# The first expert's first two tiles, filled from eight of sixteen token tiles and run among the convolution's end and the routing

## The reference

```
x = x + conv(ln_c(x))        # 3 causal depthwise convolutions (3, 7, 15 taps), mixed 96 -> 32 by w_mix
t = tokens(x)                # 4 x 512 tokens of 512 features
t = t + moe(layernorm(t))
moe: probs = softmax(x @ gate_w.T); the 2 best of 8 experts, their weights normalised to 1
     h = silu(x @ w1[e]) * (x @ w3[e])    # 512 -> 1024
     y = h @ w2[e]                        # 1024 -> 512, times the gate, summed over the token's experts
```

## Time and profile before

| | |
|---|---|
| median of 3 runs | 844.46 us |
| the profiled execution: its own time | 843.52 us |
| its span, first to last instruction | 841.8 us |
| busy share of the span | PE 94%, VectorE 41%, ScalarE 37%, GpSimd 34% |
| chain that ended last | PE 87%, VectorE 8%, issue 2%, ScalarE 1% |

### The profile page before, as it was taken

The page is one execution under the profiler, slowest core; times in us unless marked ns, Lnnn a source line. Parts: engine busy times, 40 slices in busy tenths (PEclk is TensorE's granted clock), DMA queues, the critical chain, the costliest instruction groups (busy, mean ns, idle before and its releaser), DMA issues.

```text
span 841.8 us, 13004 instructions
## 1 busy us (share of the span) xinstructions
PE 789.8 (94%) x3764; PEld 655.8 (78%) x3765; DVE 347.8 (41%) x791; ACT 314.5 (37%) x487; POOL 286.4 (34%) x313
## 2 busy tenths in 40 slices
PE   4999999639999999999999999999999999999993
PEld 3777888528888888888888888888888888888882
DVE  5887658685113611262117214511361171244111
ACT  6784755433124411352126215312441262253120
POOL 4445220011324522272227215432452272154311
PEclk9999999559999999999999999999999999999997
DMA  7248678728122711272116414612271174111211
GB/s 239 46 76 150 148 153 176 265 98 328 27 35 70 278 37 25 37 285 64 34 29 221 140 25 117 244 27 36 69 280 37 25 232 129 25 25 37 31 32 25
DMA packets 55873, 91.72 MB, mean 109 GB/s; under 512 B 7344, under 2 KB 40496, under 8 KB 49712
## 3 DMA queue, kind: packets, MB, share of 16 engines
q1 hardware_dynamic: 45728, 71.64, 27.4%
q0 software_dynamic: 9408, 19.42, 12.5%
q10 hardware_dynamic: 720, 0.46, 0.2%
HBM read 64.97 MB, written 18.15 MB: 99 GB/s over the span
## 4 chain that ended last, share of the span: by engine, by line
PE 87%; DVE 8%; issue 2%; ACT 1%; DMA 0%; POOL 0%; POOLq 0%; DVEq 0%; ACTq 0%
PE bank L720 23%; PE bank L718 23%; PE bank L719 23%; PE bank L734 4%; PE bank L631 3%; PE bank L632 3%; PE bank L633 3%; PE bank L712 2%; PE bank L653 1%; DVE bn L782 1%; DVE wc_lo L823 1%; DVE w_lo L270 1%; PE bank L671 1%; PE bank L646 1%; DVE mv L791 1%
## 5 line engine op out<-in xcount | busy, mean ns | idle before, releaser
L718 PE MATMUL bank<-w_hi,xT_hi 128*128 128x512 f32 x576 | 228.8, 397 | 4.4 <-DVE xT_lo L1019 4.4
L720 PE MATMUL bank<-w_hi,xT_lo 128*128 128x512 f32 x576 | 225.4, 391 | 0.0
L719 PE MATMUL bank<-w_lo,xT_hi 128*128 128x512 f32 x576 | 225.0, 391 | 0.0
L1042 DVE TENSOR_TENSOR h<-bank,h 128x512 f32<-128x512 f32 x72 | 49.7, 690 | 273.1 <-PE bank L720 273.1
L718 PEld LDWEIGHTS bank<-w_hi,xT_hi 128*128 128x128 f32 x576 | 108.7, 189 | 26.3 <-DVE xT_lo L1019 4.8
L720 PEld LDWEIGHTS bank<-w_hi,xT_lo 128*128 128x128 f32 x576 | 108.5, 188 | 23.5
L719 PEld LDWEIGHTS bank<-w_lo,xT_hi 128*128 128x128 f32 x576 | 108.8, 189 | 21.7
L559 ACT ACTIVATE h<-bank 128x512 f32<-128x512 f32 x72 | 43.0, 598 | 196.6 <-PE bank L720 196.5
L718 PE MATMUL bank<-w_hi,hT_hi 128*128 128x512 f32 x288 | 115.3, 400 | 0.0
L1046 DVE TENSOR_TENSOR hT_lo<-bank,hT_hi 128x512 fp32r<-128x512 f32 x72 | 49.8, 692 | 153.8 <-ACT hT_hi L563 153.8
L720 PE MATMUL bank<-w_hi,hT_lo 128*128 128x512 f32 x288 | 113.0, 392 | 0.0
(11 more groups left out here) (145 smaller groups left out, 955.5 us busy)
## 6 DMA issues: line engine op xcount, KB each, us to landing
w_raw<-in_units SPq DMA_DIRECT2D x48, 1024.0 KB, 6.3
joint<-xs_parts SPq DMA_DIRECT2D x64, 128.0 KB, 3.9
out_x<-XT SPq DMA_DIRECT2D x17, 256.0 KB, 3.6
XT<-in_x SPq DMA_DIRECT2D x16, 256.0 KB, 6.9
xn_rows<-xnb SPq DMA_DIRECT2D x16, 256.0 KB, 2.5
xg<-xn_rows,gather_at POOLq DMA_INDIRECT x37, 3.4
out_x<-y,add_at POOLq DMA_INDIRECT x36, 4.9
gate_row<-gate_rows,gate_at POOLq DMA_INDIRECT x36, 3.3
```

What stands on the lines that cost most here:

```text
L718: pe.matmul(B[bank][:], stat_hi, hi, start=start, stop=False)
L719: pe.matmul(B[bank][:], stat_hi, lo, start=False, stop=False)
L720: return pe.matmul(B[bank][:], stat_lo, hi, start=False, stop=stop)
L1042: dve.tensor_tensor(h[:, j, :], B[2 * j + 1][:], h[:, j, :], ALU.mult).then_inc(h_out, 1)
```

## The change

The first two tiles of expert 0 (256 rows) are filled from the picks of batch 0 alone, in rank order. Where batch 0 has more than 256 picks of expert 0, as here (264), batch 1 goes on from its count; otherwise batch 1 starts at row 256. Behind the convolution TensorE's list has these two tiles written out, with the transposes, logits and routing products of batch 1 between their products. The loop begins at tile 2 and has 41 rounds in all.

- **Start.** ScalarE runs one `Sqrt` right after `ones` is made, ahead of everything else; VectorE does `wc_low(0)` and `x_low(0)` before `x_scales(1)`.
- **Steps 22 to 25.** `count(0)` moves into step 22, `rank_batch(0)` from VectorE's step 23 to 22, followed by `first_ranks()`. GpSimd makes the eight 128x128 one-hot tiles `row_first`; `first_slots()` (8 matmuls of 2 columns) runs inside step 24; `first_table()` makes the row indices; GpSimd gathers tile 0 into a buffer of its own. SyncE loads units 0, 1, 2 behind steps 21, 22, 23 into places that are free by then (`w_first`), and ScalarE makes their `w_hi` in its rounds 23 to 25.
- **Behind the convolution.** `low_half` 0, 2, 3, 4 go to GpSimd, 1 and 5 stay on VectorE; the 16 `token_rows` of batch 1 go to GpSimd as well. Tile 2's gather index is made straight after the slot table; the other tables are made on VectorE between the `gate_up` and `rest_of_hT` of tile 1.
- Both transposes of h go through PSUM bank 4; the loads of expert 1 wait for the slot table.

```diff
-TILES = NT * 2 + E - 1
+EARLY = 2
+TILES = NT * 2 + E - 1 + EARLY
...
@@ sync @@
+                if STEPS - 4 <= t < STEPS - 1:
+                    sp.wait_ge(step_ps, t)
+                    load_first(t - STEPS + 4)
+                if t == STEPS:
+                    sp.wait_ge(step_ps, STEPS)
+                    sp.wait_ge(wc_lo_out, STEPS)
+                    for k in range(IN_PLACE, UNITS):
+                        load_unit(0, k)
...
@@ gpsimd, behind its last multiply_taps @@
+            pool.wait_ge(first_ranked, 1)
+            for t in range(NT // 2):
+                ins = pool.tensor_scalar(row_first[:, t, :], iota[:], first_row[:, t:t + 1], None, ALU.is_equal)
+            ins.then_inc(first_rows, 1)
...
+            pool.wait_ge(first_ready, 1)
+            gather(first_src[:, 0:1], xg_first, xn_dram[0:NT // 2 * P, :])
+            low_half(pool, 0, 0)
+            low_half(pool, 0, 2)
+            for n in range(4):
+                pool.wait_ge(acc_st[n], 16 * NBLK // 4)
+            pool.wait_ge(spare_st, 16)
+            pool.wait_ge(xg_ps, 1)
+            gather(first_src[:, 1:2], xg, xn_dram[0:NT // 2 * P, :])
+            low_half(pool, 0, 3)
+            low_half(pool, 0, 4)
+            pool.wait_ge(ranked, 2)
+            for a in range(NT):
+                t = BATCHES[1][0] + a // 2
+                ins = pool.tensor_scalar(row_token[1][:, a, :], iota[:], rank_f[1][:, 1, a:a + 1], tokid[:, t:t + 1],
+                                         ALU.is_equal, ALU.mult)
+            ins.then_inc(rows_made, 1)
+            pool.wait_ge(gate_st, 16)
+            gather_gates(first_gate[:, 0:1])
...
+            gather(third_src[:, 0:1], xg)
+            pool.wait_ge(gate_ready, 1)
+            gather_gates(first_gate[:, 1:2])
+            pool.wait_ge(tables_ready, 1)
+            pool.wait_ge(y_out, 1)
+            add_rows(dst_i[:, 0:1])
+            pool_tile(1, 2, 3, 1)
...
@@ scalar @@
+            act.activation(rs[0][:, 0:2], eps[:], ACT.Sqrt)
...
+                if t >= STEPS - IN_PLACE:
+                    act.wait_ge(step_ps, t)
+                    high_half(act, 0, t - STEPS + IN_PLACE)
...
+            high_half(act, 0, 3)
+            silu(0, 0)
+            token_turned(NT - 1)
+            high_half(act, 0, 4)
+            silu(0, 1)
...
+            silu(1, 0)
+            act.wait_ge(acc_st[1], 16 * NBLK // 4)
+            rows_out(0)
+            silu(1, 1)
...
@@ tensor, behind the convolution @@
+            turn_tokens(1, xg_first)
+            t_moments(NT - 1)
+            logit(NT - 3)
+            pe.wait_ge(resid, NBLK - 1)
+            pe.wait_ge(xT_lo_out, 1)
+            pe.wait_ge(lo_ready[0], 1)
+            up_chunks(0, (0, 1))
+            turn(NT - 2)
+            up_chunks(0, (2, 3))
+            logit(NT - 2)
...
+            up_chunks(1, (3,))
+            up(2, 1)
+            turn_h(0, 0)
+            pe.wait_ge(lo_ready[3], 1)
+            up_chunks(3, (0, 1))
+            count(1)
+            up_chunks(3, (2, 3))
+            slots(0)
+            down_tile(0, 1)
+            pe.wait_ge(xT_lo_out, 2)
+            up(0, 1)
+            slots(1)
+            up(1, 1)
...
@@ vector, behind the convolution @@
+            for p in ended(STEPS - 1):
+                add_conv(p)
+            t_stats(NT - 1)
+            t_join(NT - 2)
+            t_scales(NT - 2)
+            xT_rest(1)
+            t_join(NT - 1)
+            low_half(dve, 0, 1)
+            t_scales(NT - 1)
             half_normal(NT - 1)
+            token_rows().then_inc(slots_hot, 1)
+            gate_up(0, 0)
             mask_batch(1)
...
+            rest_of_hT(0, 0)
             rank_batch(1)
+            gate_up(0, 1)
+            low_half(dve, 0, 5)
+            rest_of_hT(0, 1)
+            xT_rest(2)
             free_sums(range(8, NBLK))
+            hot_columns(1, 0, NT).then_inc(slots_hot, 1)
```

More of the change, by code:

```diff
@@ L74, in moment_bank, with count_bank @@
 def moment_bank(n):
-    return 7 if n % 2 and (n < 8 or n == NT - 1) else 4
+    return 5 if n == NT - 1 else 7 if n % 2 and n < 8 else 4
 def logit_bank(n):
-    return 5 if n < BATCHES[0][1] else 6
+    return 5 if n < BATCHES[0][1] else 7
+def count_bank(g):
+    return (5, 6)[g]
 def head_parts(h):
@@ L400, in _, with gather @@
                 multiply_taps(t)
-            def gather(index):
+            def gather(index, into, rows=xn_dram):
                 pool.indirect_dma_start(
-                    out=xg[:].rearrange("p q i -> p (q i)"), out_offset=None, in_=xn_dram,
+                    out=into[:].rearrange("p q i -> p (q i)"), out_offset=None, in_=rows,
                     in_offset=bass.IndirectOffsetOnAxis(ap=index, axis=0)).then_inc(xg_in, 16)
@@ L522, in _ @@
             wc_high(1)
-            for t in range(STEPS + 3):
+            for t in range(STEPS):
                 if t + 1 < NBLK:
@@ new lines, in _ @@
+            token_turned(NT - 3)
+            xT_high(1)
+            deviation(NT - 2)
+            normal(NT - 2)
+            deviation(NT - 1)
+            token_turned(NT - 2)
+            normal(NT - 1)
+            high_half(act, 0, 3)
[3 more added lines that the diff above has]
+            silu(0, 1)
+            for n in range(XB):
+                act.wait_ge(xn_st[n], 16 * NT // XB)
+            hT_high(0, 0)
+            act.wait_ge(logit_ps, NT)
@@ L547, in act_tile @@
+            silu(1, 1)
+            hT_high(1, 0)
+            hT_high(1, 1)
+            xT_high(3)
+            rows_out(1)
+            act.wait_ge(tables_ready, 1)
+            last = act.value_load(tile_last[0:1, 1:2], min_val=0, max_val=1)
+            with act.If_ne(last.val, 0):
+                for k in range(UNITS):
+                    act.wait_ge(unit_done, UNITS + (k + 1))
+                    high_half(act, 1, k)
+                act.nop()
             def act_tile(t, following):
@@ L673, in slots, with first_slots @@
                 ins.then_inc(slot_ps, 1)
+            def first_slots():
+                pe.wait_ge(first_rows, 1)
+                for t in range(NT // 2):
+                    ins = pe.matmul(B[6][:, 0:EARLY], row_first[:, t, :], first_hot[:, t, :],
+                                    start=(t == 0), stop=(t == NT // 2 - 1))
+                ins.then_inc(first_ps, 1)
             pe.wait_ge(consts, 3)
@@ new lines, in up, with turn_h, down @@
+            def up(k, split):
+                pe.wait_ge(lo_ready[k], split)
+                up_chunks(k, range(4))
+            def turn_h(t, j):
+                pe.wait_ge(h_out, t * 2 + (j + 1))
+                for c in range(4):
+                    ins = pe.transpose(B[4][:, P * c:P * c + P], h[:, j, P * c:P * c + P], ident[:])
+                ins.then_inc(hT_ps, 1)
+            def down(j, chunks):
+                for c in chunks:
+                    ins = product(7, hT_hi[:, j, c, :], hT_lo[:, j, c, :], 4 + j, c,
+                                  j == 0 and c == 0, j == 1 and c == 3)
+                return ins
@@ L871, in rank_batch @@
                 n, half = NT // 2, NT // 2 * E
-                counted = [B[7][:, P * k:P * k + half].rearrange("p (t e) -> p t e", e=E) for k in range(2)]
+                counted = [B[count_bank(g)][:, P * k:P * k + half].rearrange("p (t e) -> p t e", e=E) for k in range(2)]
                 tiles = slice(*BATCHES[g])
@@ L923, in _ @@
             x_scales(0)
-            for t in range(NS * LONG):
+            wc_low(0)
+            x_join(1)
+            x_stats(2)
+            x_low(0)
+            x_scales(1)
+            for t in range(1, NS * LONG):
                 x_join(t + 1)
```

367 lines of the change are left out of this document (203 added, 164 removed).

## The result

The changed kernel takes **840.37 us** (median of 6 runs, 838.61 to 840.98) against 844.30 (6 runs, 842.77 to 845.2): ratio 0.9954, 95% interval 0.9943 to 0.9965. It is faster by 3.9 us, where 16.4 were forecast, and lies outside the forecast's range. Its profiled execution took 839.89 us with a span of 838.2, against 843.5 and 841.8.

What follows compares the result with a forecast made beforehand. TensorE was taken to bound the kernel, with time to be had in its 41 us gap between convolution and experts. Tile 2 -14.5, start -2.4, rounds +0.5 gave -16.4 from 843.5: 827.1, forecast 828, own range 822 to 834, with rivals 813 to 838.

Steps and rivals of the forecast that it cites:

- the price of GpSimd's row makers: The 16 for slots(1) and eight row_first, 128x128 on GpSimd: 0.30 us each; at 0.45 the table comes 2 us later.
- rival 2: GpSimd's row makers (0.6 to 1.0 a piece) or the gates are slower: tile 2 at 214 to 222, 832 to 839; chance 0.18.
- rival 3: Kernel slower: row makers before slots(1) at 1.1 us a piece cancel the gain, at 1.5 the time is 852; chance 0.04.
- The start: Up to the first convolution product: earlier ScalarE table load and x_low(0) take 2.4 us off, bounds 1.3 and 3.0.
- The first product: First expert product behind the convolution: 159.7 against 187.57, before taking off the start's 2.4.
- Exclusion: VectorE instructions with two SBUF inputs and GpSimd's SBUF-reading ones exclude each other; spread loses 3.6, tile 14's scale 3.0.
- rival 1: VectorE and GpSimd pass each other: first product near 153, tile 2 at 197.5, time 814.5; chance 0.20.
- the middle of 6.2: TensorE's waits in tile 0 behind GpSimd's w_lo 3 and 4: between 4.8 and, with token_rows excluded too, 7.6.
- Tile 0: First expert product to tile 1's start: 22.6 us of TensorE's work plus 6.2 of waits, tile 1 at 188.5.
- The clock: Falls to 0.50 before tile 0, hidden by the mask wait, and before count(1), costing 1.9 us (bounds 0 and 2.4).
- The end: Two more empty rounds of the loop add 0.5 us, bounds 0 and 5.
- The gates: Written near 188.5, 4.5 us to DRAM, then fetched; y of tile 0 in time by 0.2 us if the fetch takes 4.3.

Runs made afterwards that it cites:

- The split by eight: Changed kernel with eight of batch 1's sixteen row makers moved from GpSimd to VectorE, behind hot_columns(1): 833.98 us, ratio 0.9888.
- the experiment with twelve products: Changed kernel with twelve idle 128x512 products added on TensorE ahead of the first expert product: 839.85 us, ratio 0.9955.
- the eighteen products: Changed kernel with eighteen idle 128x512 products added on TensorE ahead of its wait for GpSimd's rows: 838.19 us, ratio 0.9929.
- the fastest kernel: Changed kernel with ten of batch 1's rows and w_lo 3, 4 on VectorE, plus two edits: TILES at 39, gates ahead of batch 1's columns: 824.85 us, ratio 0.978.

## Why the prediction was wrong

**The step that failed is the price of GpSimd's row makers.** The prediction took "0.30, nearest to the select", and wrote that "nothing in the rows excludes more than 0.45". The sixteen took 1.01 each on the mean: 0.78 is the form alone, and 0.23 is the share of two instructions that VectorE shut out for 3.7 us. The prediction had that exclusion in hand, but counted only what VectorE loses by it. The trace of before also held a warning that was not shown: beside the selects of 0.29 us GpSimd has two of the same 128x128 that took 0.52 (lines 353 and 356). A form that no row showed, with two scalars from memory, was put at the price of the cheapest neighbour.

What it cost can be estimated. At 0.30 each, begun at 181.35, the rows would have ended at 186.2, before TensorE came for them at 192.7. The wait of 4.98 us and the 3.6 of lower clock behind it make 8.6 of the 10.1 us by which tile 2 missed. The split by eight, which takes away most of both, had tile 2 7.4 us earlier. The prediction's rate, 2 us per 0.1, is more than the 1.6 that sixteen instructions give, and its working does not say why; rival 2 counts it from 0.45 and rival 3 from 0.30. Rival 2 had this mechanism with 0.6 to 1.0 a piece and tile 2 at 214 to 222; on that clock it came at 218.72 + 2.2 = 220.9.

**The start**: 2.4 forecast; 2.2 in the changed kernel, 2.2 alone. Right.

**The first product**: 157.3 forecast, 157.66 measured. The convolution's last product ended at 150.08, where 150.4 - 2.4 = 148.0 was forecast, and the stalls behind it were smaller than forecast at `spread` (0.8 and not 3.6: VectorE came to it at 147.55, not at 144.6, and GpSimd was nearly through) and as forecast at tile 14's scale (3.0 and 3.0). The sum held, two of its terms only together.

**Exclusion** between a VectorE instruction that reads SBUF twice and GpSimd's subtraction holds for 4.5 us as it did for 0.9: rival 1 falls. The rule of the Trainium skill ("SBUF — State Buffer", Who interferes with whom) agrees, with 3.20 and 3.53 us where 0.16 and 0.23 were due. The last of the sixteen rows of batch 0, which reads one tile and two scalars, was shut out too, so VectorE lost 4.36 and 3.3 us, the upper case of 7.6 and not the middle of 6.2. But the forecast had put these down as waits of TensorE, and of such waits only 3.4 us are seen.

**Tile 0**: 28.8 forecast, 32.2 measured. Of TensorE's waits 0.51 and 2.93 are seen; most of the other 6.1 us above 22.6 is the lower clock, 0.52 and 0.57 in the two windows shown and 0.80 and 0.75 in the ones behind them, which the forecast had put at nothing since it "hides in the wait for the masks". For tile 2 that is nearly so, as the experiment with twelve products shows. In six profiled runs of kernels that keep GpSimd's sixteen rows as they are, tile 1 started anywhere from 185.9 to 193.0, but tile 2 20.3 to 21.2 us behind the end of the rows (17.6 with the eighteen products). So while the rows are late, what counts in tile 0 is not TensorE's pace but when VectorE is through `rank_batch(1)` (181.24), for there GpSimd's rows begin. The chain that ended last goes this way, through `nb`, the last row of batch 0 and `sel`, whose stalls are 3.0, 4.4 and 3.3 us. With the last two taken away the rows began at 179.48, 1.9 earlier.

**The clock**: 1.9 forecast in one place, behind the wait for the masks; it was 3.6 us behind another, the wait for the rows, by the experiment with eighteen products. After waits of 4.98 and 7.12 to 7.23 us the sixteen table products took 3.64 to 3.65, after waits of 1.02 to 1.46 they took 1.97 to 2.00.

**The end**: 0.5 forecast for two empty rounds, 2.3 measured, with and without them. The prediction had the bounds 0 and 5 and took the low side, with three rounds under at most 8 us as its only row; the rounds' part of those 8 us is not seen in one profile, and I took the landing for nearly all of it.

**The gates**: the prediction saw ScalarE's y "in time by 0.2 us only". While the rows were late it did not matter. With the rows in time it is the next wait, of 1.7 to 3.7 us in three kernels (VectorE's copy stands 3.54, 5.18 and 5.51 us in them), and not through y but through the low part of tile 1's `h`, which stands behind the gates' copy in VectorE's list.

What stays open: the 0.9 us between tile 2 and the last transfer, which of the two edits of the fastest kernel gave how much, and why the convolution's last product starts between 149.7 and 153.1 in profiled runs whose code up to there is the same.

## What to carry to other kernels

When a change puts an instruction form on an engine that has not run it in the trace, the price is unknown and should be bounded well above the engine's slowest neighbour of that size and not set by its cheapest: here the neighbours were 0.29 to 0.52 us and the form took 0.78. Sixteen such instructions one behind the other turn an error of 0.1 us into 1.6, so the range must reach there. Price an idle engine's work by when its result is asked for: moving the same form away brought nothing in the convolution and about 6 us where the slot table waited for it. Where two engines shut each other out, count what both lose. Work given to "free" GpSimd is free only if its duration, the stalls it gives and takes, and the wait with the lower clock behind it all fit; here six rows on it and ten on VectorE, the long subtractions on VectorE, the memory round trip started first and two empty rounds fewer turned 3.9 us into 19.

## What the runs showed of the hardware

GpSimd's `tensor_scalar` of 128x128 with one scalar from memory takes 0.58 us, with two 0.78, with two constants 0.70, when the other engines are at rest; a two-input multiply over eight such pieces at once takes 1.89. Beside a VectorE instruction that reads two tiles of SBUF one of them stands until that one is done (2.68 and 2.59 us and not 0.79), and a VectorE row of 0.33 us took 4.69 beside GpSimd's subtraction; the neighbours in the same group keep their price. So a mean over a group hides it: with the same two stalls GpSimd's share has a mean of 1.01 with sixteen rows, 1.30 with eight and 1.44 with six. The lower clock behind a wait of 4.98 us costs 3.6 us more in the traces, and products that do nothing but keep TensorE busy take it away. An empty round of this loop costs 1.13 to 1.15 us at the end of the program.
